# A raw context load issued one body earlier, three batches ahead, in the first cross-attention loop

## The reference

```python
xn = _layernorm(ctx, ln1_w, ln1_b)               # per row of the context
ln = _layernorm(latents, ln2_w, ln2_b)
q  = ln @ Wq
k, v = split(concatenate([xn, ln], axis=-2) @ Wkv)
logits = einsum('bhld,bhsd->bhls', q * scale, k * scale)    # 16 heads of 64
w   = softmax(logits)
out = einsum('bhls,bhsd->bhld', w, v) ... @ Wo
x   = x + out
```

## Time and profile before

| what | value |
|---|---|
| median of three runs | 2302.65 us (2301.64 to 2307.12) |
| the profiled execution | 2302.35 us, its span 2300.6 us |
| mean granted clock of PE | 0.951 |
| busy share of the span: PE, DVE, ACT, POOL | 89%, 72%, 58%, 25% |
| first loop | about 85 to 940 us of the span |
| second loop | about 1314 to 2110 us of the span |
| `x_raw<-in_ctx`, main DMA | 16 issues of 768 KB |

### The profile page before, as it was taken

One profiled execution on the slowest core, in us unless ns is written; L12 is line 12 of the kernel. 1 busy time (PEld: TensorE's weight loads), 2 busy tenths in 40 slices (PEclk: granted clock), 3 DMA queues, 4 the chain that ended last, 5 costly groups with the idle time before them and its releaser, 6 DMA issues. The chain is left out here.

```text
span 2300.6 us, 38264 instructions
## 1 busy us (share of the span) xinstructions
PE 2056.5 (89%) x11840; PEld 1120.5 (49%) x11840; DVE 1664.8 (72%) x4194; ACT 1343.9 (58%) x2403; POOL 567.4 (25%) x584
## 2 busy tenths in 40 slices
PE   5788979797989889988989899999999999998896
PEld 4343535353434444553366644545445454544595
DVE  5677777777767777759956678687777868685567
ACT  2266655656565747654421388787787878776202
POOL 3323333333333333107800111111112111110100
PEclk8799999999999999998999899999999999999898
DMA  3111121212121111003211211111211111110000
GB/s 120 61 60 60 61 61 60 60 60 60 60 60 60 48 57 38 23 13 112 101 36 43 67 35 35 35 35 34 49 52 34 34 34 34 34 31 1 17 11 10
DMA packets 146114, 108.78 MB, mean 47 GB/s; under 512 B 118700, under 2 KB 134040, under 8 KB 145976
## 3 DMA queue, kind: packets, MB, share of 16 engines
q1 hardware_dynamic: 145976, 107.25, 16.1%
HBM read 65.15 MB, written 14.29 MB: 35 GB/s over the span
## 5 line engine op out<-in xcount | busy, mean ns | idle before, releaser
L1087 DVE TENSOR_TENSOR x_p_lo<-x_psum,x_p_hi 128x512 f16<-128x512 f32 (+2 forms) x896 | 604.9, 682 | 194.6 <-ACT x_psum L899 194.0
L898 ACT ACTIVATE x_p_hi<-x_psum 128x512 f16<-128x512 f32 (+2 forms) x480 | 287.4, 599 | 360.5 <-PE x_psum L755 358.6
L772 PE MATMUL x_psum<-x_p_hi,x_x_both 128*128 128x512 f16 (+1 forms) x832 | 321.0, 386 | 124.7 <-DVE x_p_lo L1087 124.4
L898 ACT ACTIVATE x_p_hi<-x_psum,x_bcol 128x512 f16<-128x512 f32 (+1 forms) x416 | 292.5, 703 | 104.2 <-PE x_psum L755 102.3
L753 PE MATMUL x_psum<-x_q,x_xT_both 128*128 128x512 f16 x832 | 320.1, 385 | 0.2
L773 PE MATMUL x_psum<-x_p_lo,x_x_both 128*128 128x512 f16 (+1 forms) x832 | 319.2, 384 | 0.0
L754 PE MATMUL x_psum<-x_q,x_xT_both 128*128 128x512 f16 x832 | 318.6, 383 | 0.0
L774 PE MATMUL x_psum<-x_p_hi,x_x_both 128*128 128x512 f16 (+1 forms) x832 | 318.6, 383 | 0.0
L755 PE MATMUL x_psum<-x_q,x_xT_both 128*128 128x512 f16 x832 | 318.3, 383 | 0.0
L899 ACT ACTIVATE x_psum<-x_psum 128x512 f32<-128x512 f32 (+2 forms) x480 | 286.0, 596 | 0.6
L1033 DVE TENSOR_REDUCE x_mx<-x_psum 128x1 f32<-128x512 f32 (+2 forms) x512 | 275.6, 581 | 9.6 <-PE x_psum L817 9.1
(11 more groups left out here) (439 smaller groups left out, 3297.2 us busy)
## 6 DMA issues: line engine op xcount, KB each, us to landing
x_x_both<-context_rows SPq DMA_DIRECT2D x32, 832.0 KB, 4.6
context_rows<-x_x SPq DMA_DIRECT2D x16, 832.0 KB, 3.5
x_raw<-in_ctx SPq DMA_DIRECT2D x16, 768.0 KB
ssm_c_row<-ssm_bc_rows SPq DMA_DIRECT2D x16, 512.0 KB, 4.3
ssm_b_wide<-ssm_bc_rows SPq DMA_DIRECT2D x7, 512.0 KB, 3.4
x_mrow<-in_mask_BxS_bk SPq DMA_DIRECT2D x16, 200.1 KB
x_Wkv<-in_L_xattn_Wkv SPq DMA_DIRECT2D x4, 512.0 KB, 5.1
moe_W<-in_L_ffn_eW SPq DMA_DIRECT2D x3, 512.0 KB, 5.2
```

The costliest lines, as they stand in the source:

```text
L772: pe.matmul(out, v_hi, p_hi[r][rows, :], start=start, stop=False)
L898: act.activation(p_hi[r][rows, :], score[r][rows, :], ACT.Exp, scale=SCORE_UNIT, **bias).then_inc(p_hi_ready, 1)
L1087: v.tensor_tensor(p_lo[r][rows, :], score[r][rows, :], p_hi[r][rows, :], ALU.subtract).then_inc(p_lo_ready, 1)
```

## The change

The raw rows of batch b+3 are now loaded in body b, behind the shift row's DMA and ahead of the store of the halves of batch b+2. Before, those of batch b+2 were loaded at the head of body b. The buffer is that of batch b+1, so SP first waits until that batch is normalised. Batch 2 is loaded ahead of body 0. The last three bodies issue no raw load; for that, pair 6 is written out beside pairs 0 and 7, in both loops, and the hardware loop runs pairs 1 to 5. The title given to the change speaks of the store of the normalised rows; in the code the load stands ahead of `store_x` and behind `rows`.

```diff
-        def __init__(self, i, par, first, last):
+        def __init__(self, i, par, first, last, near):
...
             self.has_next2 = not last
+            self.has_next3 = not last and not (near and par == 1)
...
-        def pair(i, first, last):
+        def pair(i, first, last, near=False):
             for par in range(2):
-                body(At(i, par, first, last))
+                body(At(i, par, first, last, near))
         pair(0, True, False)
-        with eng.Fori(1, PAIRS - 1) as i:
+        with eng.Fori(1, PAIRS - 2) as i:
             pair(i, False, False)
+        pair(PAIRS - 2, False, False, True)
         pair(PAIRS - 1, False, True)
...
                 rows(at)
                 if not masked:
+                    sp.wait_ge(xt_ready, 1)
+                    load_raw(sp, 2, 0, 1)
                     store_x(sp, 1)
                     load_xT(sp, 1, 1)
                     load_x(sp, 1, 1)

             def body(at):
-                if at.has_next2:
-                    if masked:
-                        wait_alone(sp, bcol_ready, at.b + 1)
-                        load_mask(at.b + 2, at.par)
-                    else:
-                        sp.wait_ge(xt_ready, at.b + 1)
-                        load_raw(sp, at.b + 2, at.par, at.i + 1)
+                if at.has_next2 and masked:
+                    wait_alone(sp, bcol_ready, at.b + 1)
+                    load_mask(at.b + 2, at.par)
                 if at.has_next:
                     rows(at)
+                if at.has_next3 and not masked:
+                    sp.wait_ge(xt_ready, at.b + 2)
+                    load_raw(sp, at.b + 3, at.npar, at.ni + 1)
                 if at.has_next2:
                     if not masked:
                         store_x(sp, at.b + 2)
```

## The result

The changed kernel takes 2206.05 us in the median of four runs, the kernel before 2302.14 us; the ratio is 0.9587, 95% interval 0.9558 to 0.9615. The forecast was 2206 us. The profiled execution took 2203.91 us (span 2202.2), 98.4 us less than that of before. By the ratio the gain is 95 us (89 to 102); the forecast was 96.4.

A forecast was written before the change was run, and what follows sets the result against it. DVE's wait for late raw loads in the first context loop was taken as the bound; 105.4 - 5.6 - 4.2 - 2.0 + 2.8 = 96.4 us off 2302.35 gave 2206 us, range 2186 to 2230.

The forecast's parts named there:

- The raw load moves: First context loop: raw DMAs issued one body earlier remove DVE's raw waits, 105.4 us over 14; about 1 us stays initially.
- The odd boundary: Where the raw wait of 3.93 us goes wholly and PE regains 4.3 us through its clock: 2.8 us more over seven.
- The even boundary: At entry into a body with `par` 0, DVE's raw wait of 10.66 us goes, less 0.8 and 0.6 us.
- transposed load: Behind store and raw load it reaches PE late: 0.8 us at each of 7 even boundaries, 5.6 us, bound 2.9 each.
- refill: Without the raw wait, DVE waits for ACT's second tile: 0.6 us per even boundary, 4.2 us, bounds 0 and 1.2 each.
- clock: At even boundaries PE's lower clock after standing was taken as hidden, DVE being the bound afterwards; no gain counted.
- The first body: Before the loop, 2 us lost: raw load 1 us late and the transposed load later by as much again.
- One pair written out: Both attention stages: same instructions, one loop turn less, 0 us, bounds 1 us either way; DVE's 3.71 us wait is ACT's.
- A: Rival: looped pairs fall to the second loop's floor, 16.9 us in each of seven, 118 us, 2184 us; chance 0.10.
- B: Rival: at even boundaries the wait moves to the transposed load, 3 to 5 us at each of seven, about 2234; chance 0.12.
- C: Rival: the chain raw load, store, completion, transposed load costs more than it gives at even boundaries, 2330 us; chance 0.02.
- D: Rival: raw load still lands late, 0.8 us at each even boundary, 6 us, 2212; counted within the forecast's 0.74.

## Why the prediction was right, by its own steps

The number came right, and the mechanism in the main; but the forecast put too little on PE's wait for the transposed load, subtracted a wait that does not exist and put a gain of clock at nothing. That these three nearly cancel was luck.

*The raw load moves, 105.4 us less 1 us in the first body.* Right: 102.0 us went. Three waits of 0.9 to 1.3 us stayed, all at even boundaries that are no loop's turn (into bodies 0, 2 and 12). Why only there the runs show too: at a turn DVE starts some 2 us later, and this hides the landing; with all pairs written out the wait shows at all seven, 6.8 us.

*The odd boundary, 3.93 us and 0.4 us of clock.* Right for the pair shown: 4.49 us gained, forecast 4.3. Over all seven, taken between the shift rows of both traces, the gain is 33.4 us for 32.4 us of raw wait, so the clock gave 0.9 us net and not 2.8: before the change, two of these halves ran at a granted clock of 1.00 and took 63.2 us, and there was nothing to regain. (The prediction's own figures give 2.68 + 1.18 + 0.4 - 3.93 = 0.33 us a boundary, 2.3 us for seven.)

*The even boundary, 10.66 - 0.8 - 0.6 = 9.3 us.* Gained 8.77 in the pair shown, and 65.4 us over all seven, where the prediction's terms make 73.0 - 5.6 - 4.2 - 2.0 = 61.2 us (73.0 us are the seven raw waits there, 72.99 in the trace). Three terms were off.

The *transposed load* was mis-sized. PE waited 2.3 us for it, not 0.8: it was issued 8.6 us after the shift row (forecast 7.8, because the store landed in 5.9 us and not in 5.0), and PE wanted it 12.3 us after, not 13.05, since I had taken PE's pace from a stretch in which it ran at the lower clock after its stall. That is inside the bound of 2.9 us, but over the 2 us that the prediction itself had named as the sign that this chain was mis-sized.

The *refill* term of 0.6 us does not exist: DVE takes the second tile at 292.66 without a wait. I had read ACT's row at 321.84 as the second tile's; it is the third's, and the second had been ready since 318.84 + 0.60 = 319.44. This made good 0.6 us. ACT's timeline in the kernel before, where these are the rows of the first and the second tile:

```profile
317.86 0.58 ACT L899 ACTIVATE x_psum<-x_psum 128x512 f32<-128x512 f32 x1
...
318.84 0.60 ACT L899 ACTIVATE x_psum<-x_psum 128x512 f32<-128x512 f32 x1
```

The *clock* was put at nothing here, as hidden behind DVE. It is not wholly hidden: with the load at the head of the body, where PE stands 0.48 us, this half gains 54.40 - 42.73 = 11.67 us, 1.0 us more than the raw wait of 10.66. From the first statistics to the first `max` product PE took 337.84 - 331.70 = 6.14 us before, at the lower clock, and 5.55 us with the load at the head, its wait of 0.48 us included. The changed kernel gets this back only where its clock does not fall again.

*The first body, 2 us.* Somewhat too much: it gained 52.87 - 44.82 = 8.05 us, where the terms make 10.20 - 0.8 - 0.6 - 2.0 = 6.8. A raw wait of 1.2 us and a wait of PE of 2.5 us for the transposed load stand there.

*The added wait, 0 us.* Right: the raw issues follow the shift row at once.

*One pair written out, 0 us, bounds 1 us.* Measured by itself, 4 us less (1 to 7): at the bound or beyond it. The reason was not right either. I read DVE's wait of 3.71 us at the even boundary as one for ACT. ACT ended the tile at 317.86 + 0.58 = 318.44, 1.9 us before DVE took it, and in written-out pairs this gap is gone. Pair 6, written out in the changed kernel, took 103.60 us against 105.3 in the mean of the looped ones.

*Rivals.* A's floor was 102.2 us a pair; the kernel with the load at the head came to 102.94 us, so there was a gain beyond the forecast, but in another place of the load, not by the change itself. B was right in its mechanism and too large in its size: the wait moved to the transposed load, 2.3 us and not 3 to 5. C did not come, and D only in small: 3.4 us of raw wait stayed instead of 1. The rule of the Trainium skill (DMA: Bandwidth & Descriptors, Queues, rings and completion order) on ring order and completion agrees with these traces: the store's completion came 5.9 us after its issue behind the raw load, 8.1 us behind two such loads, 4.2 us ahead of it, and 3.8 us without it beside it.

## What to carry to other kernels

When a late load is moved earlier, look for a place behind which nobody waits: here the head of the body, three batches ahead, gave 15 us more than the slot in front of a store whose completion starts a chain. Look at what stands behind the new place in the same queue before looking at what the load itself gains. A time at which data is wanted, read from a trace behind a stall, is too late by the pace that was lost there to the lower clock. And a forecast that comes right in its sum can be wrong in its terms: here an underrated wait was paid for by a wait that did not exist and by a gain that was put at nothing.

## What was not expected of the hardware

At the turn of a hardware loop DVE's first tile started 1.9 us (before), 1.8 us (load at the head) and 2.3 us (changed) after ACT had it ready, and 4.1 us where store and raw load filled the DMA engines through the turn; in written-out pairs it started at once. ACT showed no such gap there. The traces have a few packets of a DMA queue named "instruction" in these windows (4 between 284 and 310 us of the changed kernel), so that DVE's instructions come late behind the data would fit. But the written-out pairs have such packets too, and no kernel moved them alone: that it is this is argued, not shown.
